# Block maxima of the next batch taken ahead of the second layer norm's rows on VectorE

## What is computed

```python
x = x + attention(layernorm(x))     # 16 heads of 8, blocks of 64 keys
x = x + experts(layernorm(x))       # 4 experts, 512 hidden, best 2 of 4

def attention(x):
    qkv = x @ qkv_w.T
    c = (block means of q) @ (block means of k).T * SCALE
    mask = (c >= the largest of its row) | own block
    p = softmax(where(mask, q @ k.T * SCALE, -inf))
    return (p @ v) @ proj_w.T + proj_b

def experts(x):
    logits = x @ wr + br
    gates = softmax(two best logits)
    y = gelu(x @ w1 + b1) @ w2 + b2
    return sum over the two of gates * (y - c + c_sum)   # c, c_sum: constants of b1, w2, b2
```

## Time and profile before

| what | value |
|---|---|
| runs | 973.37, 979.45 and 982.94 us; median 979.45 |
| span of the profiled execution | 979.1 us, first to last instruction |
| PE busy | 909.5 us |
| DVE busy | 555.5 us |
| ACT busy | 459.5 us |
| POOL busy | 182.8 us |

### The profile page before, as it was taken

The page is one execution under the profiler, slowest core; times in us unless marked ns, Lnnn a source line. Parts: engine busy times, 40 slices in busy tenths (PEclk is TensorE's granted clock), DMA queues, the critical chain, the costliest instruction groups (busy, mean ns, idle before and its releaser), DMA issues.

```text
span 979.1 us, 24109 instructions
## 1 busy us (share of the span) xinstructions
PE 909.5 (93%) x9572; PEld 602.9 (62%) x9572; DVE 555.5 (57%) x1552; ACT 459.5 (47%) x740; POOL 182.8 (19%) x183
## 2 busy tenths in 40 slices
PE   2794999999999999999999999999999999999995
PEld 1463676665766666666666666666666666666662
DVE  7533636667474756657474755747475665736321
ACT  1321364463736355463736455373635446373640
POOL 5601011212102121211112121220212121210211
PEclk9965779999999999999999999999999999999998
DMA  7413060533515152442516143352615243350110
GB/s 206 126 49 83 13 203 25 144 105 99 151 55 171 32 162 83 127 122 76 174 27 189 40 143 102 105 146 63 165 29 166 79 138 102 82 157 2 56 54 14
DMA packets 96021, 99.50 MB, mean 102 GB/s; under 512 B 8968, under 2 KB 82704, under 8 KB 95888
## 3 DMA queue, kind: packets, MB, share of 16 engines
q1 hardware_dynamic: 93168, 85.19, 30.9%
q0 software_dynamic: 2544, 12.58, 4.0%
q10 hardware_dynamic: 192, 0.13, 0.1%
HBM read 48.20 MB, written 28.71 MB: 79 GB/s over the span
## 4 chain that ended last, share of the span: by engine, by line
PE 66%; DVE 17%; issue 8%; ACT 5%; SPq 1%; DMA 1%; POOL 1%; DVEq 0%; POOLq 0%; ACTq 0%
PE y_ps L400 15%; PE s_ps L309 8%; PE o_ps L343 5%; PE s_ps L332 5%; PE s_ps L258 5%; PE s_ps L260 5%; DVE rmax L649 5%; PE s_ps L259 5%; ACT hid L936 4%; PE v_ps L318 2%; PE a_ps L373 2%; PE o_ps L350 2%; PE a_ps L267 2%; DVE nmax L658 2%; SPq L1107 1%
## 5 line engine op out<-in xcount | busy, mean ns | idle before, releaser
L400 PE MATMUL y_ps<-hid,w2s 128*128 128x512 f32 x480 | 243.9, 609 | 0.0
L900 ACT ACTIVATE prob<-s_ps 128x1024 f32<-128x1024 f32 x128 | 131.1, 1025 | 222.1 <-PE s_ps L332 222.1
L649 DVE TRANSPOSE_TENSOR_REDUCE rmax<-s_ps 128x16 bf16<-128x512 f32 x256 | 167.3, 691 | 65.8 <-PE s_ps L309 65.5
L936 ACT ACTIVATE hid<-s_ps,b1s 128x512 f32<-128x512 f32 x256 | 171.4, 688 | 36.8 <-PE s_ps L260 36.5
L309 PE MATMUL s_ps<-qdiag,kv 64*128 64x512 f32 x768 | 138.4, 467 | 14.9 <-DMA kv<-kv_chosen 7.5
L309 PEld LDWEIGHTS s_ps<-qdiag,kv 64*128 64x128 f32 x768 | 86.8, 257 | 43.8 <-issue 14.7
L258 PE MATMUL s_ps<-xnhi,w1hi 128*128 128x512 f32 x256 | 112.2, 438 | 1.5
L658 DVE TENSOR_REDUCE nmax<-v_ps 16x64 bf16<-16x256 bf16 x128 | 52.4, 409 | 107.4 <-PE v_ps L325 106.8
L1036 POOL TENSOR_TENSOR yT<-yT,gate_cols 128x512 f32<-128x512 f32 x48 | 61.7, 1285 | 271.4 <-DVE gate_cols L745 271.0
L893 ACT COPY vaug<-v_ps 128x128 f32<-128x128 f32 x128 | 34.0, 266 | 156.6 <-PE v_ps L318 155.8
L332 PEld LDWEIGHTS s_ps<-nmax,hone 16*128 16x128 bf16 x2048 | 69.0, 95 | 54.9 <-issue 27.5
(11 more groups left out here) (146 smaller groups left out, 1095.7 us busy)
## 6 DMA issues: line engine op xcount, KB each, us to landing
gate_cols<-gates SPq DMA_DIRECT2D x64, 256.0 KB, 5.2
kv_table<-stage SPq DMA_DIRECT2D x16, 768.0 KB, 3.9
kv<-stage SPq DMA_DIRECT2D x16, 768.0 KB, 6.2
kv_chosen<-selected SPq DMA_DIRECT2D x15, 768.0 KB, 5.3
kv<-kv_chosen SPq DMA_DIRECT2D x15, 768.0 KB, 4.9
qdiag<-qpair SPq DMA_DIRECT2D x504, 16.0 KB
xs<-in_x SPq DMA_DIRECT2D x16, 256.0 KB, 4.4
out_x<-x SPq DMA_DIRECT2D x16, 256.0 KB, 4.7
```

The source lines that it names most:

```text
L400: ins = pe.matmul(dst[:], w2s[:, n, :], hid[:, n, :], start=(c == 0), stop=(c == C - 1))
L649: v.tensor_reduce(rmax[m % 2][:, half * 8:(half + 1) * 8, :], s_ps[m % 2][:, half * N:(half + 1) * N].rearrange("p (a c) -> p a c", c=32), ...
L900: act.activation(prob[m % 2][:].rearrange("p h s -> p (h s)"), s_ps[m % 2][:], ACT.Exp, scale=SCALE).then_inc(exped, 1)
L936: act.activation(hid[:, k, :], up_ps[up_bank(k)], ACT.Gelu, bias=b1s[:, k:k + 1]).then_inc(gelued, 1)
```

## The change

In the vector program the call of `block_max(b + 1, 0)` at the end of batches 1 to 14 moves from behind `c_rows(b)` and `c_add(b - 2)` to ahead of both. No instruction is added, taken out or altered, and the other engines' programs are the same.

```diff
                 o_project(b, T - 1)
                 c_stats(b)
+                if b >= 1 and b + 1 < B:
+                    block_max(b + 1, 0)
                 c_rows(b)
                 if b >= 2:
                     c_add(b - 2)
-                if b >= 1 and b + 1 < B:
-                    block_max(b + 1, 0)
             b = B - 1
```

## The result

The changed kernel takes 998.26 us (median of 4 runs, 996.78 to 999.01), the kernel before 979.5 us in the same comparison: a ratio of 1.0196 with a 95% interval of 1.0159 to 1.0233, so it is slower by some 19 us. The span of the profiled execution went from 979.1 to 996.3 us, by 17.2. The forecast was 995.3 and slower, in a range of 987 to 1008.

A forecast was written before the change was run, and what follows sets the result against it. The prediction took PE to bound the kernel, busy 909.5 of 979.1 us. Thirteen stalls of 1.22 us make 15.9, added to the median 979.45 for 995.3 us, range 987 to 1008.

The forecast's parts named there:

- No gain: DVE at batch ends: the maxima wait for PE's scores, so their start stays and the gain is zero; chance 0.02.
- Step 1: DVE after the maxima: c_rows starts at 483.29, c_add at 484.32 and ends at 485.02, before 479.60.
- Step 2: PE's first down product of a batch waits for c_add to free its bank: starts 485.08, 1.22 us late.
- Step 3: PE's queue behind the down product comes 1.22 us late; DVE's nmax, some 1.0 late, is covered by that.
- Step 4: Who pays: 13 boundaries, batches 2 to 14; at batch 1 nmax's 0.36 us is covered by 0.41 idle.
- Step 5: SP's queue: store L1125 waits for c_add, about 1.5 us later; 17 us cover it, cost nothing.
- The cold start: PE's first matmul after the stall may take 0.27 us more: stall 1.49, or 19.4 us in all.
- The clock as a rival: PE's granted clock falls oftener at batch starts: up to 22.5 us more, 1017.8; five or more falls, chance 0.13.
- PE catching up: PE's 1.03 us idle per batch swallows most of the stall, leaving 2.5 us, 981.9; chance 0.07.

The follow-up runs named there:

- c_rows alone: On the kernel before, only c_rows moved behind the block maxima, c_add staying ahead: 979.27 us, ratio 0.9974.
- the dose: The changed kernel with c_rows' four instructions issued once more, into a spare tile, between maxima and c_rows at 13 boundaries: 1014.39 us, ratio 1.0342.

## Why the prediction was right

The forecast came out, 18.8 us by medians against 15.9 forecast, and with it the mechanism. The forecast stall itself makes 15.1 of it; that the rest, which the sum didn't hold, is small is partly luck.

- No gain: right. The idle time ahead of the maxima was forecast as 5.67 and is 5.68; the maxima wait for PE's scores in both kernels.
- Step 1, c_add's end: forecast 2.96 us after the maxima begin (485.02 - 482.06), measured 2.91 (493.25 - 490.34). c_rows takes 0.99 and not 1.03 until c_add can start.
- Step 2, the new last wait: right, at 13 boundaries, ended by L752, with a hand-over of 0.06. The stall was forecast as 1.22 and is 1.10 in the wait and 1.16 in the length of a batch; 13 of these are 15.1, not 15.9. So the sum had it too long by 0.06, most of it c_add's early end of step 1.
- Step 3, nmax covered: right; it starts 2.83 us behind the maxima (2.9 forecast). With c_rows alone its delay of 0.33 costs 0.03 a batch, and the full delay costs nothing where the down product stands further back.
- Step 4, batch 1 free: right, 55.11 against 55.12.
- Step 5, the store: issued at 493.28 just behind c_add, and nothing in the changed kernel's trace waits for it. With the down product further back it comes as late, and nothing is lost.
- The cold start of up to 0.27: 0.06 of it at most. The down product takes 1.12 us on the chain against 1.06, and its weight load stood with it until c_add was done. That agrees with the row of before in which a load waits with its matmul; in this program the wait for `bank_y.free` stands ahead of both. The rule of the Trainium skill (TensorE: Matmul & The Clock Gate, section "Step-by-step: what each phase is for"), that loads can be drawn ahead, gave nothing here, where the load itself waits.
- The clock as a rival: not seen in the two profiles of the changed kernel; falls were seen with a stall twice as long.
- PE catching up, the second rival: out, by batches of 56.7 in place of 55.5 to 56.2 and by the dose.

What the sum left out is the scatter of single executions: late keys, a fall of the clock and a slower start added 2.7 - 1.7 + 1.2 = 2.2 us to this profile. The difference of the medians is another 1.6 us above that of the spans. Most of that lies in which execution of the kernel before was profiled. In every execution that has both on record, the time is 1.6 to 2.1 us above the span, so the 0.35 by which the prediction got from span to median was no such distance. By an estimate from these, the profiled execution took some 980.8 us, 1.3 above the median of 979.5; the profiled one of the changed kernel took 998.04, 0.2 below its median. With the kernel measured a second time the ratio was 1.0164, 16.5 us by the medians there.

## What to carry to other kernels

An idle engine's time ahead of a wait is where its own bookkeeping should stand: moving work from before a wait to behind it gains nothing unless that work holds up the awaited instruction, and it puts the work into the stretch where others wait for this engine. Before moving a step, look for what it releases: here it was not the moved result that mattered but a bank that c_add frees, wanted by an instruction at the head of another engine's queue. The price is what the moved work exceeds the other engine's lead by, so two steps of which one fits and the other nearly does can cost a full microsecond together.

## What was not expected

The granted clock fell for some 14 us in a single batch of the kernel with the longer stall. That batch took 64.31 - 57.77 = 6.5 us more than an ordinary one, of which late keys are 0.6. The clock fell for shorter stretches at two other boundaries of that execution, while four other executions of the same kernel come out within 0.7 us of each other. Thirteen stalls of 1.1 us in the changed kernel left the clock at 1.00.
